# One-hot rows of a routing table: wide compares replaced by one narrow instruction per column

## What is computed

```python
gate_logits = x_flat @ gate_w.T                      # 4096 tokens, 8 experts
topk_vals, topk_idx = jax.lax.top_k(gate_logits, 2)
topk_w = jax.nn.softmax(topk_vals, axis=-1)
comb = comb.at[jnp.arange(T)[:, None], topk_idx].add(topk_w)
for e in range(8):
    h = gelu(x_flat @ w1[e].T + b1[e], approximate=False)
    out = out + comb[:, e:e + 1] * (h @ w2[e].T + b2[e])
```

## Time and profile before

| | |
|---|---|
| three runs, us | 2081.46, 2082.64, 2082.74; median 2082.64 |
| the profiled execution, us | 2077.95 |
| its span, us | 2076.1 |
| its mean granted TensorE clock | 0.924 |
| busy over the span: TensorE, VectorE, GpSimd, ScalarE | 77%, 67%, 51%, 40% |
| instructions of VectorE counted as busy | 1482 |

### The profile page before, as it was taken

One profiled execution on the slowest core, in us unless ns is written; L12 is line 12 of the kernel. 1 busy time (PEld: TensorE's weight loads), 2 busy tenths in 40 slices (PEclk: granted clock), 3 DMA queues, 4 the chain that ended last, 5 costly groups with the idle time before them and its releaser, 6 DMA issues. The chain is left out here.

```text
span 2076.1 us, 22252 instructions
## 1 busy us (share of the span) xinstructions
PE 1594.2 (77%) x5692; PEld 891.2 (43%) x5693; DVE 1389.0 (67%) x1482; ACT 829.7 (40%) x1496; POOL 1061.4 (51%) x676
## 2 busy tenths in 40 slices
PE   5377778867777867677876777572999999999991
PEld 2122225522224542223452222351676767676760
DVE  2799997689997689998779999637222222222225
ACT  7444436635333754442663533230222222323222
POOL 0799880389893359896149988100223232322210
PEclk9699999979999979999989999785999999999995
DMA  3265540255461146552027555712101011110107
GB/s 112 76 238 199 194 141 21 79 206 207 167 210 43 39 162 204 201 200 86 21 95 246 199 175 173 309 65 82 36 30 35 31 33 33 33 33 32 34 21 265
DMA packets 77416, 247.42 MB, mean 119 GB/s; under 512 B 10812, under 2 KB 24517, under 8 KB 72454
## 3 DMA queue, kind: packets, MB, share of 16 engines
q1 hardware_dynamic: 70502, 227.69, 31.4%
q0 software_dynamic: 6816, 18.62, 2.8%
HBM read 220.72 MB, written 23.99 MB: 118 GB/s over the span
## 5 line engine op out<-in xcount | busy, mean ns | idle before, releaser
L390 PE MATMUL psum<-HC_sb,ident_sb 128*128 128x512 f32 x1024 | 494.2, 607 | 65.1 <-DVE HC_sb L1362 56.8
L390 PE MATMUL psum<-experts_sb 64*128 64x512 f32 (+5 forms) x962 | 313.5, 550 | 232.4 <-DVE HC_sb L1362 144.3
L952 ACT ACTIVATE psum<-experts_sb 128x1024 f32<-128x1024 f32 x256 | 285.4, 1117 | 508.5 <-DVE experts_sb L1352 395.4
L1352 DVE TENSOR_TENSOR_SCAN experts_sb<-psum,DBX_sb 128x1024 f32<-128x1024 f32 x172 | 389.8, 2276 | 32.3 <-POOL DBX_sb L1042 31.3
L390 PEld LDWEIGHTS psum<-HC_sb,ident_sb 128*128 128x128 f32 x1024 | 190.5, 192 | 282.4 <-issue 132.3
L390 PEld LDWEIGHTS psum<-experts_sb 64*128 64x128 f32 (+5 forms) x962 | 98.2, 152 | 469.4 <-DVE HC_sb L1362 239.3
L1738 ACT ACTIVATE hgt_sb<-psum_moe,b_sb 128x128 f32<-128x128 f32 x568 | 154.6, 383 | 359.1 <-PE psum_moe L1688 359.0
L1651 PE MATMUL psum_moe<-experts_sb,hgt_sb 128*128 x1136 | 259.4, 382 | 4.2 <-ACT hgt_sb L1738 2.8
L1651 PE MATMUL psum_moe<-experts_sb,XGT_sb 128*128 x568 | 257.6, 597 | 0.3 <-issue 0.3
L1621 POOL DMA_INDIRECT y_rows<-YS_sb,iy_sb x71 | 70.8, 998 | 356.9 <-PE psum_moe L1672 221.9
L1651 PEld LDWEIGHTS psum_moe<-experts_sb,hgt_sb 128*128 128x128 f32 x1136 | 216.4, 191 | 66.7 <-issue 40.7
(11 more groups left out here) (253 smaller groups left out, 1914.7 us busy)
## 6 DMA issues: line engine op xcount, KB each, us to landing
DA_sb<-bc_rows SPq DMA_DIRECT2D x128, 512.0 KB, 4.6
experts_sb<-bc_rows SPq DMA_DIRECT2D x64, 512.0 KB, 3.7
SQ_sb<-bc_rows SPq DMA_DIRECT2D x64, 512.0 KB, 4.2
X_XT_sb<-bc_rows SPq DMA_DIRECT2D x64, 512.0 KB, 5.4
experts_sb<-w1T SPq DMA_DIRECT2D x8, 1024.0 KB, 19.4
experts_sb<-w2T SPq DMA_DIRECT2D x8, 1024.0 KB, 21.4
experts_sb<-y_rows SPq DMA_DIRECT2D x8, 1024.0 KB, 11.8
X_sb<-x_tok SPq DMA_DIRECT2D x5, 1024.0 KB, 7.0
```

The source lines that it names most:

```text
L390: return nc.tensor.matmul(o, lhsT, rhs, start=start, stop=stop, **k)
L952: nc.scalar.activation(decays[i % 2], DT[:, c, :], ACT.Exp, scale=a_neg[:, s:s + 1]).then_inc(da_ready, 1)
L1352: v.tensor_tensor_scan(STATE[i % STATE_SLOTS], decays[i % 2], DRIVE[i % STATE_SLOTS], 0.0, ALU.mult, ALU.add).then_inc(h_ready, 1)
```

## The change

The cast of `iota_p` to a bfloat16 row `iota_b` is added as a `step` after R_CHOSEN (so R_ALL is 43). `TILE1` and the semaphore `onehot_tile` go. `OLO` is built with one `tensor_scalar` for each of the eight columns of a group, which compares `iota_b` with that column of LO, one value per partition. `OHI` is built with two `tensor_scalar` for each column, which compare with HI and multiply: by the immediate 128 q + 4096, and by the partition number, a second value per partition. Only the last instruction of each eight or sixteen increments `onehot_ready`.

```diff
--- before.py
+++ after.py
@@ -46,7 +46,7 @@
 TAIL = RING * (NT // RING - 1) + 1
 TOK = B * L
 Y_ROWS = 3 * TOK + NT * P
-R_DIF, R_CHOSEN, R_ALL = 14, 15, 42
+R_DIF, R_CHOSEN, R_ALL = 14, 15, 43
 
 
 def on_pool(i):
@@ -1553,7 +1553,7 @@
         HGT = sb("hgt", [P, HB, P])
 
         OLO = HG[:, :].bitcast(BF16).rearrange("p (g k m) -> p g k m", g=2, k=8)
-        TILE1 = HGT[:, :, :].rearrange("p k m -> p (k m)").bitcast(BF16)[:, 0:16 * NT].rearrange("p (g k t) -> p g k t", g=2, k=8)
+        iota_b = sb("iota_b", [P, P], BF16)
         OHI = sb("ohi", [P, 2, 8, 2, NT], BF16)
         IX = sb("ix", [P, RING], U32)
         XG = sb("XG", [P, RING, C])
@@ -1570,7 +1570,7 @@
 
         c_loaded = sem("c_loaded"); x3_loaded = sem("x3_loaded")
         route = sem("route"); route_exp = sem("route_exp"); rank_ready = sem("rank_ready")
-        onehot_ready = sem("onehot_ready"); onehot_used = sem("onehot_used"); onehot_tile = sem("onehot_tile"); tab_step = sem("tab_step"); tab_done = sem("tab_done")
+        onehot_ready = sem("onehot_ready"); onehot_used = sem("onehot_used"); tab_step = sem("tab_step"); tab_done = sem("tab_done")
         ix_ready = sem("ix_ready"); indices_there = sem("indices_there")
         xg_ready = [sem(f"xg_ready{k}") for k in range(RING)]
         t1_ready = sem("t1_ready"); xgt_done = sem("xgt_done"); m1_ready = sem("m1_ready"); hg_done = sem("hg_done")
@@ -1786,6 +1786,7 @@
             step(v.tensor_tensor(LG2[:, :, :], OH1[:, :, :], OH2[:, :, :], ALU.add))
             assert done[0] == R_CHOSEN
 
+            step(v.tensor_copy(iota_b[:, :], iota_p[:, :]))
             dve.wait_ge(rank_ready, 1)
             step(v.tensor_copy(TOT[:, :, :].rearrange("p e n -> p n e"),
                                psum[:, 1, 0:NG_ * E].rearrange("p (n e) -> p n e", n=NG_)))
@@ -1821,18 +1822,19 @@
             step(v.tensor_tensor(P2[:, :], EX[:, :], P1[:, :], ALU.mult))
             assert done[0] == R_ALL
             lo, hi = (x[:, :, :].rearrange("p j n -> p (j n)") for x in (LO, HI))
-            tok = token[:, :, :, :].rearrange("p j n i -> p (j n) i")
             for g in range(8):
-                s = slice(8 * g, 8 * g + 8)
                 if g >= 2:
                     dve.wait_ge(onehot_used, g - 1)
-                v.tensor_tensor(OLO[:, g % 2, :, :], iota_p[:, :].unsqueeze(1).broadcast_to((P, 8, P)),
-                                lo[:, s].unsqueeze(2).broadcast_to((P, 8, P)), ALU.is_equal).then_inc(onehot_ready, 1)
-                v.tensor_tensor(TILE1[:, g % 2, :, :], iota_p[:, 0:NT].unsqueeze(1).broadcast_to((P, 8, NT)),
-                                hi[:, s].unsqueeze(2).broadcast_to((P, 8, NT)), ALU.is_equal).then_inc(onehot_tile, 1)
-                dve.wait_ge(onehot_tile, g + 1)
-                v.tensor_tensor(OHI[:, g % 2, :, :, :], TILE1[:, g % 2, :, :].unsqueeze(2).broadcast_to((P, 8, 2, NT)),
-                                tok[:, s, :].unsqueeze(3).broadcast_to((P, 8, 2, NT)), ALU.mult).then_inc(onehot_ready, 1)
+                for k in range(8):
+                    q = 8 * g + k
+                    i = v.tensor_scalar(OLO[:, g % 2, k, :], iota_b[:, :], lo[:, q:q + 1], None, ALU.is_equal)
+                i.then_inc(onehot_ready, 1)
+                for k in range(8):
+                    q = 8 * g + k
+                    v.tensor_scalar(OHI[:, g % 2, k, 0, :], iota_b[:, 0:NT], hi[:, q:q + 1], float(P * q + TOK), ALU.is_equal, ALU.mult)
+                    i = v.tensor_scalar(OHI[:, g % 2, k, 1, :], iota_b[:, 0:NT], hi[:, q:q + 1], token[:, 0, 0, 1:2], ALU.is_equal,
+                                        ALU.mult)
+                i.then_inc(onehot_ready, 1)
             dve.wait_ge(onehot_used, 8)
             table = [0]
```

## The result

| | before | after |
|---|---|---|
| median of 8 runs, us | 2082.46 | 2087.51 |
| lowest and highest, us | 2080.41 and 2086.73 | 2085.13 and 2092.04 |
| span of the profiled execution, us | 2076.1 | 2084.7 |
| instructions of VectorE counted as busy | 1482 | 1651 |

A forecast was written before the change was run, and what follows sets the result against it. VectorE was taken to bound the routing loop; fixed times, streams and second pointers summed to 3.20 us per group against 3.171, +0.2 us over eight groups, on the 2082.64 us median: 2082.8 us, range 2078 to 2090.

The forecast's parts named there:

- the sum: Routing loop, new instructions' fixed times, streams and second pointers: 3.20 us per group against 3.171, +0.2 us over eight groups.
- the prediction's own sign: Profile after, TensorE's bursts: the forecast is wrong if they lie more than 0.5 us off the old distance.
- second sign: VectorE's distances in the loop: near 165 and 140 ns favour rival 2 (30 ns apart) or rival 3 (14 apart).
- rival 3: Loop's narrow instructions: a pointer costs its steady price, 130 ns fixed; +5.4 us, 2088.1 us; chance 0.10.
- What bounds the kernel: Routing loop, 1416.7 to 1442.2 us: VectorE sets 3.171 us per group, and any change reaches the end one for one.
- The cast: Once, before the loop, 128x128 float32 to bfloat16, 227 ns: inside VectorE's 2.2 us wait for the rank matmuls, costing nothing.
- Streaming: New loop instructions: 33 ns for 128 elements and 19 for 71, the middle between 0 and 67 or 37.
- Rival 2: Loop's streams run at two elements a step, not at the middle; +4.7 us, 2087.3 us; chance 0.15.
- Fixed time with a pointer: Each narrow loop instruction: 103 ns start to start less streaming, a queue hiding most of the pointer's cost; ends 103 and 130.
- Second pointer: Eight instructions of each group: 20 ns extra each, ends 0 and 60.
- Rival 1: Loop's narrow instructions: the pointer is free in a queue, fixed time 66 ns; -8.2 us, 2074.5 us; chance 0.13.
- Rival 4: VectorE is fed too slowly with 168 more instructions; gaps of 20 ns each give +3.8 us; chance 0.05.

The follow-up runs named there:

- e3: The changed kernel with the compares reading the float32 row instead of the bfloat16 one; TensorE's bursts 4.700 us apart, against 4.149 for the change.
- e10: The changed kernel plus eleven chains of six repeats behind its loop, 128 float32 elements; tensor_scalar with a pointer 196 ns alone, 170 behind aggregates.
- e7: The kernel before, wide instructions all in bfloat16, column index innermost, OLO between TILE1 and OHI; 2.09 us per group, ratio to before 0.9952.
- e8: Like e7, but only pairs of columns innermost and the partition number multiplied in by a tensor_scalar; 1.609 us per group, ratio to before 0.9945.
- e2: The changed kernel plus ten chains of extra VectorE instructions behind its loop; 128 bfloat16 elements take 102 ns without a pointer, 162 with one, 222 with two.

## Why the prediction was right or wrong

**The time lies in the range, but the sum that stands behind the forecast does not hold.** No change was forecast with 0.60 and slower with 0.26; it came out slower by 0.28%, 2087.5 us against a forecast of 2082.8 and a range of 2078 to 2090. The sum gave +0.2 us for the loop and the trace shows +7.8. That the time still lies in the range is due to the room that the range left for the rivals, not to the sum. By the prediction's own sign, bursts more than 0.5 us off the old distance, the forecast is wrong: they are 0.98 us off. Its second sign points at the right rival: distances near 165 and 140 ns that differ by 14 ns between 128 and 71 elements speak for rival 3, and 162.5 and 148 were measured.

*What bounds the kernel*: right. VectorE is busy through the whole loop, TensorE's burst is unchanged, and a group's longer distance reaches the end one for one within what the timing can tell (7.8 us by the loop, 3.5 to 8.3 by the ratio).

*The cast*: right, it lies in the wait for the rank matmuls.

*Streaming*: right, with luck. The rows gave only the bounds 0 and 67 ns (0 and 37 for 71 elements), and the middle was a choice; 33 and 19 ns are what was measured. Rival 2 (two elements at a time) falls; e3 shows what it would have looked like.

*Fixed time with a pointer*: this step failed. The prediction took 103 ns with the words that a queue of short instructions hides the most of it. It is 129 ns in the loop and in every chain of tensor_scalar, however short its neighbours. The two rows put aside as not like the new queue, 137 and 123 ns, enclose it. This is rival 3, at its price of 130: 24 x 26 ns = 0.62 us per group, 5.0 us in all. e10 shows why the lowest row was no price.

*Second pointer*: mis-sized. 20 ns were taken between ends of 0 and 60; the upper end is right, 60 to 61 ns. 8 x 40 = 0.32 us per group, 2.6 us in all.

The two terms make the whole of the 7.8 - 0.2 = 7.6 us by which the sum missed. Had both been taken at their upper ends, with the streaming as it was, the sum would have been 8 x 163 + 8 x 149 + 8 x 209 = 4.17 us per group, against 4.149.

*Rival 1* (the pointer is free in a queue) falls, with the cost line that it leaned on: the Trainium skill (VectorE: DVE Perf Modes, "The TRN2 errata") gives VectorE 58 cycles plus the elements over the factor, by estimate about 60 ns of fixed time, and no term for a pointer. Measured are 68 ns without one, near to the rule, and 129 with one. The same section's advice against many small tiles held: the loop's fixed times went from about 0.2 us per group to 3.6. *Rival 4* falls: in the chains starts follow each other 88 and 71 ns apart, so VectorE is fed fast enough for distances of 148 ns and more, and a compare costs the same there as in the loop.

## What to carry to other kernels

Price an instruction of VectorE by the distance between starts in a run of its own kind, and count its pointer scalars: here 68 ns, plus 60 for each, plus the stream. Where n narrow instructions replace a wide one, the streaming must win back their n fixed times, pointers included, less the one of the wide instruction; here that was 3.6 against 0.2 us per group. A better way was to keep it wide, with 2-byte elements throughout and an innermost dimension that every operand steps through, and with a step of 4 bytes, not 16, for what TensorE reads as its moving operand. A single short distance next to instructions of another kind can be paid for by the neighbour; sum over a whole period before taking it as a price.

## What was not expected of the hardware

- In the chains of e10 a BATCH_NORM_AGGREGATE that follows another kind of instruction has a distance of 89 to 92 ns in place of 66 (99 behind a wait), and the instruction behind the last one is 23 to 26 ns short: starts seem to be shifted, sums are not. Why is open.
- A matmul whose moving operand of 142 bfloat16 columns has a step of 16 bytes, its weights strided too, is followed by the next after 258 ns (e7); in the kernel before it is 119 ns. At a step of 4 bytes nothing was lost (119 ns, e8), all at the 1.2 GHz level of the clock (granted 0.50 in this stage). Other steps and the 2.4 GHz level were not tried.
- Outputs that begin at an odd multiple of 2 bytes cost VectorE nothing: 148 ns for 71 elements at either start (L1834 in the loop, chain 10 of e2). The Trainium skill (Vector Engine (DVE) Microarchitecture Reference, "Performance modes — why throughput varies by op and dtype") says that 4-byte alignment makes no difference, and the trace agrees.
